# Attention rounds with one value quarter and one relative quarter each, single maxima, and fewer relative columns in the second group of steps

## The chip, the cores and the metric

One Trainium2 chip, one core of it. The metric is the device time of one execution in microseconds. A change of less than 0.2% can't be told from no change by the runs shown here.

## The reference, cut to what matters

Input x is 16 sequences of 512 rows with 128 features. The layer is pre-norm attention with 16 heads of width 8, and after it a shared and expert feed-forward part. All in float32.

```python
rel_pos = arange(L)[None, :] - arange(L)[:, None] + (MAX_LEN - 1)      # L = 512, MAX_LEN = 128
rel_k, rel_v = relative_k[rel_pos], relative_v[rel_pos]                # table of 255 rows; an index is clipped
scores = einsum('bhld,bhrd->bhlr', Q, K) * scale + einsum('bhld,lrd->bhlr', Q, rel_k)
attn = softmax(scores)
out = einsum('bhlr,bhrd->bhld', attn, V) + einsum('bhlr,lrd->bhld', attn, rel_v)
x = x + out @ Wo.T + bo
x = x + ffn(layernorm(x))      # 2 shared and 8 experts, top 2
```

The table has 255 rows, and an index beyond its end takes the last row. So every key that lies 127 or more ahead of a query's row takes the table's last row: such a key is called far, all others near. For a query in rows 0 to 127 all keys from 256 on are far, for rows 128 to 255 all keys from 384 on; for later queries no block of 128 keys is far as a whole.

## The kernel before, in words

Attention works on a pair of sequences at a time (8 pairs), and within a pair in 16 steps of 32 query rows. A step is 8 quads: a quad is 4 query rows of both sequences and all 16 heads, which is 128 partitions by 512 keys of scores in one PSUM bank. A step has two rounds (j = 0 and 1) of 4 quads in banks 0 to 3. Four steps share a group (`s // GROUP_STEPS`), since they share which key blocks are far: steps 0 to 3 are group 0, 4 to 7 group 1, and so on (the change's title counts from one, so its "group two" is group 1 here). A round is written (s, j) below.

In a round TensorE does in this order (`score_round`, L1287):

1. the scores of four quads: `low_terms` (L1198, two quads at a time on halves of the rows), then per two quads `first_terms` (L1182) for both and `relative_terms` (L1190) for both. Each is four matmuls on the four column quarters of the array, and the last of `relative_terms` counts up `score_done`;
2. products of an earlier step into bank 7 (`AV_BANK`): in j = 0 `relative_products` of step s - 2 (both halves), in j = 1 `value_products` of step s - 1 (both sequences). Columns 0 to 255 of the bank hold the value products, 256 to 511 the relative ones. `relative_products` has as many key blocks as are near: 2 in group 0, 3 in group 1, else 4;
3. in some rounds a piece of the work for the next pair (`AHEAD`: transposed rows in (8, 0) and (8, 1), keys in step 9, queries in 11, natural queries in 12, relative queries in (14, 1) and (15, 0)) or of this pair (`OWN`: values in (0, 1) and (1, 0)), through bank 1 or banks 0 and 1;
4. in j = 1 the transpose of the reduced relative result of step s - 2, into columns 256 to 383 of bank 7;
5. the transposes of the probabilities of the round before (16 of 128 x 128, L1248). The last of them waits (`next_scores_wait`, L1116) until banks 0 to 3 are free for the next scores: all four exponentials of this round done, a piece read, and the first transposed bank copied out.

VectorE takes the maxima of the round (`maxima`, L785: one quad, one quad, then two quads in one instruction), in j = 0 then a copy of transposed probabilities, the two maskings of bank 7 (`mask_products`, L799), another copy and `reduce_relative`; in j = 1 `reduce_values`, `rel_out` and two copies. It has work for the next pair behind these in some rounds: statistics in (4, 1) and (5, 1), variances in (6, 0), normalising in step 7, key and query parts from (10, 1) to (14, 0). ScalarE does the four exponentials (L579) and two copies (L568). GpSimd spreads the queries into masked stationary operands one step ahead. Each engine runs this order as written out; semaphores are the only link.

SP issues for each step the load of `rv_step` (`value_window`, L302, 512 KB, one buffer, free again once `av_done` of the step before is up), then the stores of `rel_t`; before step 11 it adds the copies of keys, and before step 14 those of queries (`copy_queries`, L316), which wait for GpSimd and for ScalarE's and VectorE's splits.

`k_hi`, `k_lo`, `k_both` and `k_swap` hold per sequence the 512 plain keys in columns 0 to 511 and behind them the 256 far ones (blocks 2 and 3 with the table's last row added). `near_keys` and `columns` (L1176, L1179) read in group 0 the plain blocks 0 and 1 and then the far ones, as two stretches; all other groups read the 512 plain ones. `relative_terms` streams 256 columns in group 0 and 512 in all others. `value_products` reads `v_far` (values with the table's last row added) for far blocks, in group 1 too.

After the last pair comes `last_step` (L1332) and then the feed-forward part of all 16 sequences.

Of the kernel before, what the change touches and what calls it, by code (L numbers as in the profile page):

```python
# [45 lines left out]
MAXIMA = 3  # L46
# [13 lines left out]
NEAR_GROUP = RT - FAR  # L60
# [27 lines left out]
def attention_ffn(nc, x, w_qkv, cols, rows, wo_t, bo, rk_win, rv_win, rw, rb, w1, w2, b2,  # L88
                  sw1, sw2, sb2, b1_cols, consts, rel_scratch, out):
    with ExitStack() as ctx:  # L90
# [173 lines left out]
        def _(sp):  # L264
# [74 lines left out]
            def pair_windows(pair, parity, first, ahead):  # L339
# [181 lines left out]
        def _(act):  # L521
# [11 lines left out]
            def high_keys(pair, parity, b):  # L533

                act.wait_ge(k_ready, START + pair * 2 + b + 1)
                plain = q_f[:, b * L:(b + 1) * L]
                nc.scalar.activation(k_hi[parity][:, b, 0:L], plain, ACT.Identity, bias=bks_col[:, 0:1])
                nc.scalar.activation(k_hi[parity][:, b, L:KEYS], plain[:, FAR * P:L], ACT.Identity, bias=bk_far_col[:, 0:1]).then_inc(hi_ready, 1)
# [31 lines left out]
            def exponentials(pair, parity, s, j, first):  # L570
# [131 lines left out]
        def _(dve):  # L702
# [42 lines left out]
            def low_keys(pair, parity, b):  # L745
# [3 lines left out]
                nc.vector.scalar_tensor_tensor(k_lo[:, b, 0:L], plain, bks_col[:, 0:1], k_hi[parity][:, b, 0:L], ALU.add, ALU.subtract)  # L749
                nc.vector.scalar_tensor_tensor(k_lo[:, b, L:KEYS], plain[:, FAR * P:L], bk_far_col[:, 0:1], k_hi[parity][:, b, L:KEYS],  # L750
# [71 lines left out]
            def rel_out(pair, s):  # L822
# [4 lines left out]
                nc.vector.tensor_copy(rel_t[:, s % 2, :], ps[0:64, AV_BANK, 2 * P:3 * P]).then_inc(rel_t_ready, 1)  # L827
# [254 lines left out]
        def _(pe):  # L1082
# [93 lines left out]
            def near_keys(rows, group):  # L1176
                return rows.rearrange("k (a c) -> k a c", c=FAR * P)[:, 0::2, :] if group == 0 else rows[:, 0:L]

            def columns(rows, group):  # L1179
                return rows.rearrange("p (a c) -> p a c", c=FAR * P) if group == 0 else rows  # L1180

            def first_terms(parity, s, q):  # L1182
                group = s // GROUP_STEPS
                for b in range(2):
                    for half in range(2):
                        at = b * 64 + half * 32
                        nc.tensor.matmul(columns(ps[at:at + 32, q % IN_ROUND, :], group), stat_hi[s % 2][:, half, b, q, :],  # L1187
                                         near_keys(k_both[parity][:, half, b, :], group), start=False, stop=False, skip_group_check=True)

            def relative_terms(s, q):  # L1190
                near = FAR * P if s // GROUP_STEPS == 0 else L
                window = L - QT - ROWS * s - QT * q
                for g in range(4):
                    last = nc.tensor.matmul(ps[32 * g:32 * g + 32, q % IN_ROUND, 0:near], stat_rel[s % 2][:, q, g, :, :].rearrange("k l h -> k (l h)"),  # L1194
# [3 lines left out]
            def low_terms(parity, s, p):  # L1198

                group = s // GROUP_STEPS  # L1200
                for q, source in ((2 * p, k_hi[parity]), (2 * p + 1, k_swap[parity])):
                    for b in range(2):
                        for half in range(2):
                            at, row = b * 64 + half * 32, 64 * (half ^ (q % 2))
                            nc.tensor.matmul(columns(ps[at:at + 32, q % IN_ROUND, :], group), stat_lo[s % 2][row:row + 64, b, q, :],  # L1205
                                             near_keys(source[row:row + 64, b, :], group), start=True, stop=False, skip_group_check=True)

            def scores(parity, s, j):
# [3 lines left out]
                for p in duos:  # L1212
                    for q in (2 * p, 2 * p + 1):
# [341 lines left out]
```

## Time and profile before

| what | value |
|---|---|
| median of 3 runs | 2220.38 us (2219.79 to 2220.86) |
| the profiled execution: its time | 2220.67 us |
| its span, first to last instruction | 2218.6 us |
| mean granted TensorE clock | 0.990 |
| TensorE busy | 2116.2 us (95%) |
| VectorE busy | 1700.0 us (77%) |
| ScalarE busy | 1522.2 us (69%) |
| GpSimd busy | 1059.8 us (48%) |
| attention rounds | about 44 us to 1676 us of the span |

The span and the time differ by 2.1 us, so what is saved within the span is saved in the time. A TensorE matmul row counts to its modelled end, so "busy" says little; the weight loads (PEld) have real starts, and the start of a round is the start of its first load of `low_terms` (L1205). Times in rows of a timeline are from the start of the span.

### The profile page before, as it was taken

The page shows a single profiled execution, that of the slowest core. Times are in us where ns is not written, and L with a number is a line of the kernel's source. Part 1 is how long each engine was busy: PE and PEld are TensorE (multiplying, and loading weights), DVE is VectorE, ACT ScalarE, POOL GpSimd, SP SyncE. Part 2 cuts the span into 40 slices and gives each one's busy share as a digit, 9 for nine tenths or more (in the row PEclk, how much of TensorE's full clock was granted, in tenths as well). Part 3 has the DMA queues.
Part 4 walks back from the last instruction along what each step waited for, and adds up shares of the span by engine and source line. Part 5 has one row for each costly group of instructions (what it writes and reads, how often), then busy time and mean ns, then how long its engine had stood idle before and what let it go on. Part 6 is the DMA issues. An engine that isn't in the chain of part 4 may idle for free.

```text
span 2218.6 us, 87983 instructions
## 1 busy us (share of the span) xinstructions
PE 2116.2 (95%) x37442; PEld 1547.3 (70%) x37442; DVE 1700.0 (77%) x3703; ACT 1522.2 (69%) x3290; POOL 1059.8 (48%) x992
## 2 busy tenths in 40 slices
PE   3999999999999999999999999999998999999998
PEld 1667767676677667767776777777776777777776
DVE  4787887888788888888787888788875676766665
ACT  3666666666666666666666666666665888888887
POOL 2444344345334433443444335334332777776776
PEclk7999999999999999999999999999999999999999
DMA  5112211321221122112212211222112122122110
GB/s 135 32 53 65 71 53 43 83 58 47 65 71 53 46 70 73 43 53 73 62 53 59 76 53 43 64 62 62 53 43 40 22 24 28 19 28 24 27 21 11
DMA packets 255678, 114.46 MB, mean 52 GB/s; under 512 B 142218, under 2 KB 251156, under 8 KB 255348
## 3 DMA queue, kind: packets, MB, share of 16 engines
q1 hardware_dynamic: 255348, 109.60, 20.5%
q8 instruction: 264, 4.33, 0.8%
q14 instruction: 66, 0.54, 0.1%
HBM read 83.34 MB, written 8.39 MB: 41 GB/s over the span
## 4 chain that ended last, share of the span: by engine, by line
PE 67%; DVE 15%; ACT 9%; issue 4%; POOL 3%; SPq 1%; DMA 0%; ACTq 0%; POOLq 0%; DVEq 0%
PE ps L1248 14%; PE ps L1187 9%; PE ps L1265 9%; PE ps L1194 7%; DVE neg_max L789 6%; PE ps L1205 6%; PE ps L1277 5%; ACT probs L579 4%; POOL probs_t L500 3%; DVE probs_t L795 3%; ACT probs L646 2%; PE ps L1431 2%; PE ps L1414 2%; PE ps L1416 2%; PE ps L1415 2%
## 5 line engine op out<-in xcount | busy, mean ns | idle before, releaser
L579 ACT ACTIVATE probs<-ps,neg_max 128x512 f32<-128x512 f32 x1024 | 694.3, 683 | 467.2 <-DVE neg_max L789 467.2
L789 DVE TENSOR_REDUCE neg_max<-ps 128x1 f32<-128x512 f32 (+1 forms) x768 | 619.1, 861 | 157.8 <-PE ps L1194 157.4
L439 POOL TENSOR_TENSOR stat_hi<-q_twice,mask8h 128x1024 f16<-128x1024 f16 x128 | 243.6, 1903 | 879.2 <-PE ps L1194 773.2
L1248 PE MATMUL ps<-const,probs 128*128 128x128 f32 x4096 | 513.7, 275 | 33.8 <-DVE probs_t L795 18.4
L1248 PEld LDWEIGHTS ps<-const,probs 128*128 128x128 f32 x4096 | 455.8, 142 | 84.0 <-ACT probs L579 36.5
L795 DVE COPY probs_t<-ps 128x512 f32<-128x512 f32 x512 | 339.9, 684 | 89.2 <-PE ps L1248 86.5
L500 POOL TENSOR_TENSOR probs_t<-probs,probs_t 128x1024 f16<-128x1024 f32 x160 | 340.1, 2134 | 109.0 <-ACT probs_t L652 109.0
L568 ACT ACTIVATE probs_t<-ps 128x512 f32<-128x512 f32 x512 | 283.9, 595 | 96.4 <-PE ps L1248 95.4
L1187 PE MATMUL ps<-keys,stat_hi 128*32 128x512 f16 x4096 | 314.4, 383 | 0.0
L1194 PE MATMUL ps<-rk_split,stat_rel 96*32 96x512 f16 (+1 forms) x4096 | 284.3, 353 | 0.0
L999 DVE SCALAR_TENSOR_TENSOR keys<-ps,comb,keys 128x128 f32<-128x128 f32 x640 | 179.8, 344 | 129.3 <-PE ps L1433 129.3
L455 POOL TENSOR_TENSOR stat_rel<-q_rel,mask4h 96x1024 f16<-96x1024 f16 x128 | 250.6, 1958 | 34.1 <-DVE q_rel L774 34.1
L646 ACT ACTIVATE probs<-ps,b_s 128x512 f32<-128x512 f32 x320 | 205.2, 683 | 54.0 <-PE ps L1416 50.7
L1431 PE MATMUL ps<-w_h,probs_t 128*128 128x128 f16 x1280 | 222.8, 219 | 5.2 <-DVE keys L999 1.8
L1433 PE MATMUL ps<-w_h,probs_t 128*128 128x128 f16 x1280 | 222.6, 219 | 0.0
L1432 PE MATMUL ps<-w_l,probs_t 128*128 128x128 f16 x1280 | 222.6, 219 | 0.0
L1265 PE MATMUL ps<-probs_t,v_s 128*32 128x128 f32 x6656 | 215.5, 272 | 0.0
L1277 PE MATMUL ps<-probs_t,rv_step 128*32 128x128 f32 x6656 | 204.1, 272 | 0.0
L579 ACT ACTIVATION_READ_ACCUMULATOR probs<-ps,neg_max 128x1 f32 x1024 | 200.7, 196 | 0.0
L1265 PEld LDWEIGHTS ps<-probs_t,v_s 128*32 128x32 f32 x6656 | 184.9, 110 | 20.3 <-issue 0.2
L1277 PEld LDWEIGHTS ps<-probs_t,rv_step 128*32 128x32 f32 x6656 | 183.9, 110 | 20.2 <-issue 0.2
L1187 PEld LDWEIGHTS ps<-keys,stat_hi 128*32 128x32 f16 x4096 | 85.4, 95 | 151.0 <-issue 107.6
(136 smaller groups left out, 2867.4 us busy)
## 6 DMA issues: line engine op xcount, KB each, us to landing
rv_step<-in_rv_win SPq DMA_DIRECT2D x128, 512.0 KB, 3.8
keys<-keys SPq DMA_DIRECT2D x64, 96.0 KB, 2.3
x_pair<-in_x SPq DMA_DIRECT2D x8, 512.0 KB, 4.3
q_twice<-q_hi SPq DMA_DIRECT2D x32, 128.0 KB, 2.4
q_lo_pair<-q_lo SPq DMA_DIRECT2D x32, 128.0 KB, 2.4
rel_scratch<-rel_t SPq DMA_DIRECT2D x256, 16.0 KB, 3.2
x_pair<-in_x SPq DMA_DIRECT2D x16, 256.0 KB, 3.0
x_pair<-rel_scratch SPq DMA_DIRECT2D x64, 64.0 KB, 3.9
```

The source lines that it names most:

```text
L455: nc.gpsimd.tensor_tensor(stat_rel[s % 2][:].rearrange("k q g l h -> k (q g) l h"), quads.unsqueeze(2).broadcast_to([REL_K, QUADS * 4, QT, ...
L500: nc.gpsimd.tensor_tensor(hid_l[:, n % SLOTS, :, :], hid[:, n % 2, :, :], hid_h[:, n % SLOTS, :, :], ALU.subtract).then_inc(hid_low, 1)
L568: nc.scalar.activation(probs_t[s % 2][:, q, :, :].rearrange("p r c -> p (r c)"), ps[:, tr_bank(q, piece), :], ACT.Copy).then_inc(evac_act, 1)
L579: nc.scalar.activation(probs[:, q, :], ps[:, i, :], ACT.Exp, bias=neg_max[:, q:q + 1], accum_out=row_sum[parity][:, s * QUADS + q:s * QUAD ...
L789: nc.vector.tensor_reduce(neg_max[:, IN_ROUND * j + at:IN_ROUND * j + at + n], ps[:, at:at + n, :], op=ALU.max, axis=AX_X, negate=True).th ...
L795: nc.vector.tensor_copy(probs_t[s % 2][:, q, :, :].rearrange("p r c -> p (r c)"), ps[:, tr_bank(q, piece), :]).then_inc(evac_dve, 1)
L1187: nc.tensor.matmul(columns(ps[at:at + 32, q % IN_ROUND, :], group), stat_hi[s % 2][:, half, b, q, :], near_keys(k_both[parity][:, half, b, ...
L1194: last = nc.tensor.matmul(ps[32 * g:32 * g + 32, q % IN_ROUND, 0:near], stat_rel[s % 2][:, q, g, :, :].rearrange("k l h -> k (l h)"), rk_s ...
L1248: last = nc.tensor.transpose(ps[:, bank, rt * P:(rt + 1) * P], probs[:, q, rt * P:(rt + 1) * P], ident)
L1265: nc.tensor.matmul(ps[32 * g:32 * g + 32, AV_BANK, b * P:(b + 1) * P], values[:, 32 * g:32 * g + 32], cols, start=rt == 0, stop=rt == RT - ...
L1277: last = nc.tensor.matmul(ps[32 * g:32 * g + 32, AV_BANK, (2 + half) * P:(3 + half) * P], rv_step[:, RT - 1 - rt, q * 32:q * 32 + 32], pro ...
L1431: nc.tensor.matmul(y, hid_h[:, place, k, rows], w2_h[:, e, k, :], start=k == 0, stop=False)
```

## The change: what it does, and the diff

- `maxima` takes the four quads of a round one by one, four instructions instead of three, and each exponential waits for its own.
- Keys are laid with the far ones first: far 2, far 3, plain 0 to 3. Group 0 reads the columns from 0, group 1 those from 128 (far 3, plain 0 to 2), later groups those from 256, always 512 in one stretch. So the quads of groups 0 and 1 have the far keys first in the bank, and `relative_terms` writes the last columns: 256 in group 0, 384 in group 1 (before 512), 512 later. The key blocks in `value_products` and `relative_products` are counted accordingly; their number is as before.
- In group 0 the first two quads of a round go first, relative, first, relative.
- The products: round (s, 0) does the value products of sequence 1 and the relative half 1 of step s - 2, round (s, 1) the value products of sequence 0 and the relative half 0 of step s - 1. `av_done` comes in (s, 0) as before. The wait for the landed window is now in (s, 1). `last_step` is rearranged in the same way.
- The transpose of the reduced relative result goes to columns 384 to 511 of bank 7.
- SP issues `copy_queries` in step 14 behind the window and the stores.

```diff
-                    if ahead and s == STEPS - 2:
-                        copy_queries(pair + 1, False)
                     if s:
                         value_window(pair, s - 1)
...
                             copy_keys(pair + 1, 1 - parity, b)
+                    if ahead and s == STEPS - 2:
+                        copy_queries(pair + 1, False)
...
-                    if i < MAXIMA:
-                        act.wait_ge(max_done, START + ((pair * STEPS + s) * ROUNDS + j) * MAXIMA + i + 1)
+                    act.wait_ge(max_done, START + pair * TILES + s * QUADS + q + 1)
...
-                for at, n in ((0, 1), (1, 1), (2, 2)):
-                    dve.wait_ge(score_done, START + pair * TILES + s * QUADS + IN_ROUND * j + at + n)
-                    nc.vector.tensor_reduce(neg_max[:, IN_ROUND * j + at:IN_ROUND * j + at + n], ps[:, at:at + n, :], op=ALU.max, axis=AX_X,
-                                            negate=True).then_inc(max_done, 1)
+                for i in range(IN_ROUND):
+                    q = IN_ROUND * j + i
+                    dve.wait_ge(score_done, START + pair * TILES + s * QUADS + q + 1)
+                    nc.vector.tensor_reduce(neg_max[:, q:q + 1], ps[:, i, :], op=ALU.max, axis=AX_X, negate=True).then_inc(max_done, 1)
...
+            def group_keys(rows, group):
+                start = min(group, RT - FAR) * P
+                return rows[:, start:start + L]
+
+            def group_blocks(group):
+                far = [(block, True) for block in range(min(RT, group + FAR), RT)]
+                return far + [(block, False) for block in range(RT - len(far))]
...
             def relative_terms(s, q):
-                near = FAR * P if s // GROUP_STEPS == 0 else L
+                near = min(RT, s // GROUP_STEPS + FAR) * P
...
                 for p in duos:
-                    for q in (2 * p, 2 * p + 1):
-                        first_terms(parity, s, q)
-                    for q in (2 * p, 2 * p + 1):
-                        relative_terms(s, q)
+                    if s < GROUP_STEPS and p % 2 == 0:
+                        for q in (2 * p, 2 * p + 1):
+                            first_terms(parity, s, q)
+                            relative_terms(s, q)
+                    else:
+                        for q in (2 * p, 2 * p + 1):
+                            first_terms(parity, s, q)
+                        for q in (2 * p, 2 * p + 1):
+                            relative_terms(s, q)
...
                     pe.wait_ge(rel_reduced, START + pair * STEPS + s)
+                else:
+                    pe.wait_ge(rel_t_ready, START + pair * STEPS + s)
...
                 scores(parity, s, j)
-                if j == 0:
-                    before, step = (pair, s - 2) if s >= 2 else (pair - 1, STEPS + s - 2)
-                    if s >= 2 or not first:
-                        for half in range(2):
-                            relative_products(before, step, half)
-                else:
-                    for b in range(2):
-                        if s:
-                            value_products(pair, s - 1, b)
-                        elif not first:
-                            value_products(pair - 1, STEPS - 1, b)
+                trailing = s - 2 + j
+                if trailing >= 0:
+                    value_products(pair, trailing, 1 - j)
+                    relative_products(pair, trailing, 1 - j)
+                elif not first:
+                    value_products(pair - 1, STEPS + trailing, 1 - j)
+                    relative_products(pair - 1, STEPS + trailing, 1 - j)
```

## Rows read from the trace of the kernel before

**Rows 1.** The page's busy time, share of the span and instructions of each engine.
```profile
PE 2116.2 (95%) x37442; PEld 1547.3 (70%) x37442; DVE 1700.0 (77%) x3703; ACT 1522.2 (69%) x3290; POOL 1059.8 (48%) x992
```

**Rows 2.** Windows: steps 6, 7, 8 of pair 3; stretch, length, busy time per engine.
```profile
733.11:744.94 11.83, 11.83 (x242) 8.51 (x242) 10.56 (x31) 7.88 (x21) 5.76 (x5) 1.00 0.17 48
744.94:756.98 12.04, 12.01 (x242) 8.54 (x241) 10.14 (x22) 7.90 (x21) 6.53 (x10) 1.00 0.17 50
756.98:770.46 13.48, 12.79 (x250) 9.38 (x249) 11.35 (x20) 8.81 (x23) 5.44 (x7) 1.00 0.16 44
```

**Rows 3.** Timeline of step 2 (group 0), pair 3: start, duration, engine, line, [idle before].
```profile
686.91 0.14 PEld L1205 LDWEIGHTS ps<-keys,stat_lo 64*32 64x32 f16 x16 [0.17 <-issue]
...
688.24 2.42 DVE L789 TENSOR_REDUCE neg_max<-ps 128x1 f32<-128x512 f32 x3 [1.25 <-PE ps L1194]
...
688.67 0.89 PEld L1277 LDWEIGHTS ps<-probs_t,rv_step 128*32 128x32 f32 x32
...
689.71 0.68 ACT L579 ACTIVATE probs<-ps,neg_max 128x512 f32<-128x512 f32 x1
689.90 0.40 SPq L307 DMA_DIRECT2D rv_step<-in_rv_win  x1
...
690.62 0.69 DVE L795 COPY probs_t<-ps 128x512 f32<-128x512 f32 x1
690.70 0.69 ACT L579 ACTIVATE probs<-ps,neg_max 128x512 f32<-128x512 f32 x1 [0.22 <-DVE neg_max L789]
...
692.20 0.14 PEld L1248 LDWEIGHTS ps<-const,probs 128*128 128x128 f32 x1 [0.65 <-ACT probs L579]
...
692.45 0.14 PEld L1205 LDWEIGHTS ps<-keys,stat_lo 64*32 64x32 f16 x16
...
696.24 1.78 PEld L1248 LDWEIGHTS ps<-const,probs 128*128 128x128 f32 x16
...
698.18 0.10 PEld L1205 LDWEIGHTS ps<-keys,stat_lo 64*32 64x32 f16 x5 [0.17 <-issue]
```

**Rows 4.** Timeline of step 4 (group 1), pair 3.
```profile
709.47 0.14 PEld L1205 LDWEIGHTS ps<-keys,stat_lo 64*32 64x32 f16 x16 [0.17 <-issue]
...
711.55 0.99 PEld L1277 LDWEIGHTS ps<-probs_t,rv_step 128*32 128x32 f32 x32
...
715.12 0.14 PEld L1205 LDWEIGHTS ps<-keys,stat_lo 64*32 64x32 f16 x16
715.68 0.12 PEld L1187 LDWEIGHTS ps<-keys,stat_hi 128*32 128x32 f16 x8 [0.42 <-issue]
...
721.28 0.14 PEld L1205 LDWEIGHTS ps<-keys,stat_lo 64*32 64x32 f16 x16 [0.17 <-issue]
```

**Rows 5.** VectorE's instructions in rows by form, 300 to 1800 us: busy, mean ns.
```profile
L789 DVE TENSOR_REDUCE neg_max<-ps 128x1 f32<-128x512 f32 x432 | 277.8, 684 | 121.5 <-PE ps L1194 121.1
L789 DVE TENSOR_REDUCE neg_max<-ps 128x2 f32<-128x1024 f32 x216 | 262.2, 1214 | 0.0
```

**Rows 6.** Timeline: rounds of pair 3 where VectorE is late or holds the bank.
```profile
673.21 1.27 DVE L795 COPY probs_t<-ps 128x512 f32<-128x512 f32 x2
...
674.26 0.14 PEld L1205 LDWEIGHTS ps<-keys,stat_lo 64*32 64x32 f16 x16
...
740.64 2.41 DVE L789 TENSOR_REDUCE neg_max<-ps 128x1 f32<-128x512 f32 x3
...
752.75 2.41 DVE L789 TENSOR_REDUCE neg_max<-ps 128x1 f32<-128x512 f32 x3
...
759.18 2.41 DVE L789 TENSOR_REDUCE neg_max<-ps 128x1 f32<-128x512 f32 x3
```

**Rows 7.** Landing of `rv_step` loads: of 26 (500 to 840 us), and of the one at 847.63.
```profile
DMA to landing us min/median/max: 3.7/3.8/4.2
DMA to landing us min/median/max: 5.1/5.1/5.1
```

**Rows 8.** Timeline of GpSimd at the change of pair.
```profile
858.52 1.96 POOL L455 TENSOR_TENSOR stat_rel<-q_rel,mask4h 96x1024 f16<-96x1024 f16 x1 [4.50 <-DVE q_rel L774]
```

More of the change, by code:

```diff
@@ L59 @@
 KEYS = L + FAR_COLS
-NEAR_GROUP = RT - FAR
 START = 1
@@ L1173, in project_values @@
                 last.then_inc(proj_done, 1)
[L1176 to L1180, printed above, removed]
+            def group_keys(rows, group):
[4 more added lines that the diff above has]
+                return far + [(block, False) for block in range(RT - len(far))]
             def first_terms(parity, s, q):
@@ L1186, in first_terms @@
                         at = b * 64 + half * 32
-                        nc.tensor.matmul(columns(ps[at:at + 32, q % IN_ROUND, :], group), stat_hi[s % 2][:, half, b, q, :],
-                                         near_keys(k_both[parity][:, half, b, :], group), start=False, stop=False, skip_group_check=True)
+                        nc.tensor.matmul(ps[at:at + 32, q % IN_ROUND, :], stat_hi[s % 2][:, half, b, q, :],
+                                         group_keys(k_both[parity][:, half, b, :], group), start=False, stop=False, skip_group_check=True)
             def relative_terms(s, q):
-                near = FAR * P if s // GROUP_STEPS == 0 else L
+                near = min(RT, s // GROUP_STEPS + FAR) * P
                 window = L - QT - ROWS * s - QT * q
                 for g in range(4):
-                    last = nc.tensor.matmul(ps[32 * g:32 * g + 32, q % IN_ROUND, 0:near], stat_rel[s % 2][:, q, g, :, :].rearrange("k l h -> k (l h)"),
+                    last = nc.tensor.matmul(ps[32 * g:32 * g + 32, q % IN_ROUND, L - near:L], stat_rel[s % 2][:, q, g, :, :].rearrange("k l h -> k (l h)"),
                                             rk_split[:, window:window + near], start=False, stop=True, skip_group_check=True)
@@ L1204, in low_terms @@
                             at, row = b * 64 + half * 32, 64 * (half ^ (q % 2))
-                            nc.tensor.matmul(columns(ps[at:at + 32, q % IN_ROUND, :], group), stat_lo[s % 2][row:row + 64, b, q, :],
-                                             near_keys(source[row:row + 64, b, :], group), start=True, stop=False, skip_group_check=True)
+                            nc.tensor.matmul(ps[at:at + 32, q % IN_ROUND, :], stat_lo[s % 2][row:row + 64, b, q, :],
+                                             group_keys(source[row:row + 64, b, :], group), start=True, stop=False, skip_group_check=True)
             def scores(parity, s, j):
@@ L1257, in value_products @@
                     pe.wait_ge(rel_reduced, START + pair * STEPS + s)
+                else:
+                    pe.wait_ge(rel_t_ready, START + pair * STEPS + s)
                 if s == 0:
                     pe.wait_ge(operands_ready, START + pair * 6 + 5 + b)
-                for rt in range(RT):
+                for rt, (block, far) in enumerate(group_blocks(group)):
                     for g in range(4):
@@ L1263, in value_products @@
                         cols = probs_t[s % 2][:, :, rt, at:at + 32].rearrange("p q (l h) -> p q l h", l=QT)[:, :, :, (g % 2) * 4:(g % 2) * 4 + 4]
-                        values = v_s[:, b * 4 + rt, :] if rt < group + FAR else v_far[:, b, rt - FAR, :]
+                        values = v_far[:, b, block - FAR, :] if far else v_s[:, b * 4 + block, :]
                         nc.tensor.matmul(ps[32 * g:32 * g + 32, AV_BANK, b * P:(b + 1) * P], values[:, 32 * g:32 * g + 32], cols,
@@ L1270, in relative_products @@
                 if half == 0:
-                    pe.wait_ge(rel_t_ready, START + pair * STEPS + s)
                     pe.wait_ge(rv_landed, START + (pair * STEPS + s + 1) * 16)
-                for rt in range(near):
+                for block in range(near):
                     for g in range(4):
                         q = half * 4 + g
-                        last = nc.tensor.matmul(ps[32 * g:32 * g + 32, AV_BANK, (2 + half) * P:(3 + half) * P], rv_step[:, RT - 1 - rt, q * 32:q * 32 + 32],
-                                                probs_t[s % 2][:, q, rt, :], start=rt == 0, stop=rt == near - 1, skip_group_check=True)
+                        last = nc.tensor.matmul(ps[32 * g:32 * g + 32, AV_BANK, (2 + half) * P:(3 + half) * P], rv_step[:, RT - 1 - block, q * 32:q * 32 + 32],
+                                                probs_t[s % 2][:, q, RT - near + block, :], start=block == 0, stop=block == near - 1, skip_group_check=True)
                 if half == 1:
@@ L1333, in last_step @@
                 s = STEPS - 1
-                for half in range(2):
-                    relative_products(pair, s - 1, half)
+                value_products(pair, s - 1, 1)
+                relative_products(pair, s - 1, 1)
                 transposes(pair, s, 1, False, None)
@@ L1339, in last_step @@
                 prepare_attention(0, 0, 0)
-                for b in range(2):
-                    value_products(pair, s, b)
+                value_products(pair, s, 0)
+                relative_products(pair, s, 0)
                 rel_transposes(pair, s - 1)
@@ L1344, in last_step @@
                 prepare_output(0)
-                for half in range(2):
-                    relative_products(pair, s, half)
+                value_products(pair, s, 1)
+                relative_products(pair, s, 1)
                 prepare_h(0)
```

13 lines of the change are left out of this document (6 added, 7 removed).

## The prediction

> **What bounds the kernel now.** First the busy line: TensorE is called 95% busy [rows 1], but its ends are modelled, so I went to the starts of rounds instead. The seven pairs after the first keep one rhythm, so pair 3 stands for all. The windows give step lengths [rows 2], and in the timeline of a step the reader should look at what stands just ahead of the next round's first load. In round (2, 0) it is ScalarE: the last transpose stood 0.65 us for the last exponential [rows 3]. In (2, 1) nothing is waited for but 0.17 us of issue: TensorE's own stream sets the round. So the two rounds of a step are unequal: one short of TensorE work and set by maxima and exponentials, the other set by TensorE.
>
> TensorE's stream, from loads [rows 3, 4]. Scores take 688.67 - 686.91 = 1.76 us in group 0 (256 relative columns) and 711.55 - 709.47 = 2.08 with 512. Value and relative loads take 0.89 us per 32, thus 0.028 each; right after 512-column scores 32 take 0.99. A value quarter is 32 loads, a relative half 8 per near block. Then 0.20 of issue, and from the first transpose to the next round 698.18 - 696.24 = 1.94; j = 1 has 0.06 more for the small transpose. Check: (2, 1) = 1.76 + 64 x 0.0277 + 0.20 + 0.06 + 1.94 = 5.73, and the rows say 698.18 - 692.45 = 5.73. (4, 1): 2.08 + 1.87 + 0.26 + 1.94 = 6.15; the rows say 6.16.
>
> The other chain: let T be the first maximum's start after the round's. (2, 0) has T = 1.33 and length 5.54, so T + 4.21. Inside it exponential 1 starts at T + 1.47, but exponential 2 at T + 2.46, for it waits 0.22 us for the double maximum [rows 3].
>
> **The change, part by part.**
>
> *Single maxima.* Two single ones take 0.60 to the next start and 0.68 to the end, 1.28 against 1.21 for the double one [rows 3, 5]: VectorE pays 0.07 a round, 256 x 0.07 = 18 us if it were always on the path. The exponentials gain: number 2 follows number 1 at T + 1.47 + 0.67 = T + 2.14 instead of T + 2.46. So this chain becomes T + 3.9.
>
> *384 columns.* 32 quads of group 1 per pair lose 128 columns on four matmuls side by side. Group 0 gives the price of 256 columns: scores and the first 32 loads behind them take 1.76 + 0.89 = 2.65 there and 2.08 + 0.99 = 3.07 with 512 [rows 3, 4]. Half of the 0.42 is 0.21 a round; 64 rounds, 13 us as far as TensorE sets the round, nothing where it doesn't. Scores and 32 loads of group 1 then take 2.86, scores alone about 1.9.
>
> *Products.* Each round now has 32 value loads and 16, 24 or 32 relative ones. TensorE's floor in group 0 is 1.76 + 48 x 0.028 + 0.20 + 1.94 = 5.23 (j = 0) and 5.29 (j = 1); in group 1 with two near blocks 2.86 + 16 x 0.028 + 0.20 + 1.94 = 5.45 and 5.51, with three (24 loads more instead of 16) 5.67 and 5.73. Groups 2 and 3 keep 64 loads in each round: nothing.
>
> Next, whether VectorE lets these floors stand. In j = 0 it copies when the first transposes are in: 690.62 - 689.56 = 1.06 after the last product load [rows 3], about 0.9 where TensorE goes on after 0.2, and it is free for the next maxima 2.4 us later. New (2, 0): product loads end at 3.09, so copy at 3.99, free at 6.4, which is T = 1.17 in (2, 1): chain T + 3.9 = 5.1, below 5.29. In j = 1 the first copy starts at T + 3.0 (four maxima 2.41, `reduce_values` 0.38, `rel_out` 0.20), and from that copy to the next round it is 674.26 - 673.21 = 1.05 where it holds the bank [rows 6]: T + 4.05 = 5.2 in (2, 1) and 5.4 in (4, 1). Both just hold.
>
> Per pair, lengths before to after:
> - (1, 1) 5.73 to 5.36 (T is about 1.3 there, after the value pieces, an estimate); (2, 0) and (3, 0) 5.54 to 5.23; (2, 1) and (3, 1) 5.73 to 5.29: -0.37 - 0.62 - 0.88 = -1.87. (0, 0) to (1, 0) still carry products of the pair before with four near blocks, 64 loads: nothing.
> - (4, 0), (5, 0) 5.66 to 5.45; (4, 1) 6.16 to 5.51; (5, 1) 6.16 to 5.73: -1.50. (6, 0), (7, 0): 5.66 to 5.67, since they get 56 loads for 48. (6, 1): VectorE comes late from the variances, at a place that TensorE's transposes in (6, 0) fix and that stays; from the maxima to the end of the round it is 744.94 - 740.64 = 4.30 [rows 2, 6], now 4.05. (7, 1), behind normalising, likewise 756.98 - 752.75 = 4.23 to 4.05. Together -1.91.
> - (8, 0): VectorE's own work from the maxima of (7, 1) to these is 759.18 - 752.75 = 6.43 [rows 6], now 6.50 because of the fourth maximum. So (8, 0) pays back what (7, 1) gave and 0.07: +0.25. (8, 1) 56 loads for 64, -0.21; (9, 0) 56 for 48, +0.22. In (13, 0) and (13, 1) the exponentials end the round behind late maxima: -0.3. Together -0.04; pieces in 11, 12, 14 and 15 wait for VectorE at an unchanged place.
>
> Sum -3.82 for seven pairs, -26.7. The last pair has no work for a next one: (6, 1) and (7, 1) reach 5.73 (from 6.17), group 1 gives -2.4, total about -4.25. In all -31. Of this TensorE's removed columns are at most 13; the rest is levelling. The feed-forward part is untouched. 2220.7 - 31 = 2190, and as the profiled execution lies 0.3 above the median, 2190 also against that.
>
> *The transpose's new place and SP's order.* `rel_out` of step s - 2 is done in (s, 1) at about T + 2.8, the new wait in (s + 1, 0) comes 2 us into the next round: nothing. `copy_queries` behind the window starts at about 843 instead of 838.6; its low half waits for VectorE until 845 anyway. GpSimd's spread then ends some 0.3 later, and behind it stands an idle of 4.50 us for `q_rel` [rows 8], which covers it; without the cover it would be 7 x 0.3 = 2 us. Were the order left, the window would be asked for at 847.6 and needed at 846: the move is needed by the new place of `relative_products`.
>
> *The window itself.* SP issues it 0.34 after the last load of the relative products (688.67 + 0.89 to 689.90 [rows 3]). Before, it had a whole step. Now in group 0: last load at 3.09, issue 3.43, landing 3.8 later [rows 7], 7.23; wanted at 5.23 + 1.76 + 0.89 = 7.88. Spare 0.64 us in group 0, likewise 0.78 in group 1 and 0.98 in the rest. The bounds: 3.7 to 4.2 among 26, so nothing; 5.1 behind other traffic, and all at that, 32 x 0.66 + 32 x 0.52 + 64 x 0.32 = 58 us. I take 0, since 4.2 still fits and nothing is queued ahead of it at its new time.
>
> *First, relative, first, relative* in group 0 brings two more changes between 128-row and 96-row matmuls per round. The first maximum can start 0.2 sooner; the chain isn't the limit then, so 0. Where a change of shape costs, the rows show 0.17 to 0.20, and 0.42 from 64-row to 128-row loads [rows 4]; between L1187 and L1194 they show no idle. Bounds 0 and 64 x 2 x 0.42 = 54 us; I take 0.
>
> The Trainium skill, "TensorEngine Tiling (Array Packing)", section Key Properties, says that changing the tiling mode drains TensorE. The trace agrees for 64 to 128 rows (0.42); it doesn't say whether 96 rows are a mode of their own. If they are, 54 us come on top by it and the sum is 2244, else 2190; it is rival C that prices this from rows.
>
> **Rivals.**
> A. *The window decides* (the other side). Place: the first relative product of every (s, 1). It costs from a landing of 4.4 us on and outweighs the gain from about 4.9 (128 x 1.085 - 108 = 31 us). With 5.1 everywhere: 2190 + 58 = 2248. For: one buffer, and one row of 5.1. Against: 26 others of at most 4.2.
> B. *VectorE decides in more rounds.* Step 2 has it at 9.2 us of what will be 10.5, step 6 at 10.6 of 11.6 [rows 2]; maxima that start 0.25 late in the eight rounds j = 1 of groups 0 and 1 cost 8 x 8 x 0.25 = 16: 2206.
> C. *Drains* in group 0: 2 x 0.2 a round, 64 rounds, 26 us: 2216; by 0.42, 2244.
> D. *More gain.* (6, 1), (7, 1) reach TensorE's floor of 5.73 and (8, 0) doesn't pay back: 0.2 + 0.5 + 0.25, times 7: 2183.
>
> **How the numbers follow.** Chances: forecast 0.56 (2186 to 2196), D 0.14, B 0.18, C 0.05 (half of it slower), A 0.07. Predicted 2190. The range goes from D's end to past B, 2181 to 2210; outside lie A, C and a little more. Under 0.2% (4.4 us) the runs can't tell a change. Faster 0.89; same 0.03, from A or C partly true; slower 0.08.
>
> **What would show it.** Right: (2, 0) at 5.2 and (2, 1) at 5.3 in starts of L1205, exponentials without the 0.22 gap, (4, 1) at 5.5, (8, 0) at 7.1, group 3 as before, feed-forward the same. A shows as idle of the relative matmuls with a DMA as releaser; B as transposes waiting for VectorE's copy in j = 1; C as issue idle between first and relative loads in steps 0 to 3. Wrong altogether if a release that I have off the path (stat_ready, `rel_t_ready`) stands in front of many rounds.

## The result, and the profile after

The changed kernel takes 2184.41 us (median of 4 runs, 2182.88 to 2186.30), the one before beside it 2220.09 (2218.94 to 2220.86). The ratio is 0.984, 95% interval 0.9823 to 0.9857: faster by 36 us. Forecast were 2190 and 31 us: the time lies inside the stated range of 2181 to 2210, and 1.6 us below the narrower band of 2186 to 2196 that had the chance of 0.56.

First the page of the kernel after: the busy line, which answers to [rows 1], and the shares of the chain that ended last, after and then before.

```profile
PE 2092.8 (96%) x37442; PEld 1546.1 (71%) x37442; DVE 1704.3 (78%) x3959; ACT 1502.6 (69%) x3290; POOL 1059.9 (49%) x992
...
PE 74%; DVE 9%; ACT 7%; issue 4%; POOL 3%; SPq 1%; DMA 1%; ACTq 0%; POOLq 0%; DVEq 0%
```

```profile
PE 67%; DVE 15%; ACT 9%; issue 4%; POOL 3%; SPq 1%; DMA 0%; ACTq 0%; POOLq 0%; DVEq 0%
```

The busy line hardly moves, with 256 VectorE instructions more and no matmul fewer. The chain says what happened: TensorE's share is up by 7 points, VectorE's is down by 6 and ScalarE's by 2. The span fell from 2218.6 to 2183.6 us.

The same step 2 of pair 3 as in [rows 3], in the timeline of the kernel after, first the weight loads, then VectorE:

```profile
671.13 0.14 PEld L1204 LDWEIGHTS ps<-keys,stat_lo 64*32 64x32 f16 x16
...
672.90 0.45 PEld L1273 LDWEIGHTS ps<-probs_t,v_far 128*32 128x32 f32 x16
673.34 0.45 PEld L1273 LDWEIGHTS ps<-probs_t,v_s 128*32 128x32 f32 x16
673.77 0.45 PEld L1283 LDWEIGHTS ps<-probs_t,rv_step 128*32 128x32 f32 x16
674.42 1.73 PEld L1253 LDWEIGHTS ps<-const,probs 128*128 128x128 f32 x16 [0.20 <-issue]
676.32 0.14 PEld L1204 LDWEIGHTS ps<-keys,stat_lo 64*32 64x32 f16 x16 [0.16 <-issue]
...
681.61 0.14 PEld L1204 LDWEIGHTS ps<-keys,stat_lo 64*32 64x32 f16 x16 [0.17 <-issue]
```

```profile
672.25 2.48 DVE L786 TENSOR_REDUCE neg_max<-ps 128x1 f32<-128x512 f32 x4 [0.90 <-PE ps L1193]
675.12 0.69 DVE L791 COPY probs_t<-ps 128x512 f32<-128x512 f32 x1 [0.38 <-PE ps L1253]
...
677.50 2.48 DVE L786 TENSOR_REDUCE neg_max<-ps 128x1 f32<-128x512 f32 x4
679.89 0.47 DVE L807 TENSOR_REDUCE attn_t<-v_masked 128x32 f32<-128x128 f32 x2
```

(2, 0) is 676.32 - 671.13 = 5.19 us, before 5.54; the 0.65 us ahead of its last transpose is gone, and 16 transposes run in one go to the 0.16 of issue. (2, 1) is 5.29, before 5.73. The first maximum starts at T = 1.12 and 1.18 (T as in the prediction: from the start of the round to its first maximum). The scores take 672.90 - 671.13 = 1.77 us with the new order of first and relative terms, 1.76 before.

From the starts of `low_terms` the length of every round can be listed. Medians over pairs 1 to 6, us; rounds not shown differ by 0.01 or less:

| round | before | forecast | after |
|---|---|---|---|
| (1, 1) | 5.73 | 5.36 | 5.33 |
| (2, 0), (3, 0) | 5.54 | 5.23 | 5.19 |
| (2, 1), (3, 1) | 5.73 | 5.29 | 5.30 |
| (4, 0), (5, 0) | 5.66 | 5.45 | 5.40 |
| (4, 1) | 6.16 | 5.51 | 5.51 |
| (5, 1) | 6.16 | 5.73 | 5.72 |
| (6, 0), (7, 0) | 5.66 | 5.67 | 5.62 |
| (6, 1) | 6.16 | 5.91 | 5.96 |
| (7, 1) | 6.39 | 6.2 | 6.22 |
| (8, 0) | 6.89 | 7.14 | 6.75 |
| (8, 1) | 6.60 | 6.39 | 6.37 |
| (9, 0) | 6.53 | 6.75 | 6.74 |
| (13, 0), (13, 1), (14, 0) | 18.93 | 18.6 | 18.57 |
| a pair | 204.67 | 200.85 | 200.14 |

And there is one wait that was not there before. The waits of the kernel after, and SP's issues around it, in the last pair:

```profile
PEld ps L1283 <- DMA rv_step<-in_rv_win: 2.8, 1, 2.8
```

```profile
1475.55 0.40 SPq L305 DMA_DIRECT2D rv_step<-in_rv_win  x1
1476.45 0.84 SPq L312 DMA_DIRECT2D rel_scratch<-rel_t  x2
1481.24 0.41 SPq L380 DMA_DIRECT2D x_pair<-in_x  x1
1481.69 5.70 SPq L382 DMA_DIRECT2D x_pair<-rel_scratch  x4
1487.44 1.28 SPq L305 DMA_DIRECT2D rv_step<-in_rv_win  x1
```

`first_rel` waits until 1481.24 for the last store of the pair before and then holds SP for 6.2 us. The window comes only at 1487.44, it lands 5.7 us later, and the relative products of (3, 1) stand 2.8 us for it: that round takes 8.00 us in the last pair, for 5.30 in the others.

### The profile page after: what moved, and what is told of

The parts are those of the page before. It is cut to its first block, busy times and chain, and to the rows that moved or that the text cites. A ratio compares the mean times of both kernels' runs of the same rounds, so it can differ in the third digit from the quotient of the medians.

```text
span 2183.6 us, 88119 instructions
## 1 busy us (share of the span) xinstructions
PE 2092.8 (96%) x37442; PEld 1546.1 (71%) x37442; DVE 1704.3 (78%) x3959; ACT 1502.6 (69%) x3290; POOL 1059.9 (49%) x992
## 3 DMA queue, kind: packets, MB, share of 16 engines
HBM read 83.34 MB, written 8.39 MB: 42 GB/s over the span
## 4 chain that ended last, share of the span: by engine, by line
PE 74%; DVE 9%; ACT 7%; issue 4%; POOL 3%; SPq 1%; DMA 1%; ACTq 0%; POOLq 0%; DVEq 0%
PE ps L1253 17%; PE ps L1186 10%; PE ps L1273 9%; PE ps L1283 7%; PE ps L1193 7%; PE ps L1204 6%; POOL probs_t L498 3%; DVE probs_t L791 2%; ACT probs L643 2%; ACT probs L576 2%; PE ps L1434 2%; PE ps L1417 2%; PE ps L1419 2%; PE ps L1418 2%; PE ps L1435 2%
## 5 line engine op out<-in xcount | busy, mean ns | idle before, releaser
L786 DVE TENSOR_REDUCE neg_max<-ps 128x1 f32<-128x512 f32 x1024 | 635.5, 683 | 123.6 <-PE ps L1193 120.9
L1253 PE MATMUL ps<-const,probs 128*128 128x128 f32 x4096 | 506.1, 275 | 21.5 <-DVE probs_t L791 20.2
L1253 PEld LDWEIGHTS ps<-const,probs 128*128 128x128 f32 x4096 | 454.0, 142 | 62.4 <-issue 26.8
L1193 PE MATMUL ps<-rk_split,stat_rel 96*32 96x512 f16 (+2 forms) x4096 | 281.5, 340 | 0.0
L1283 PE MATMUL ps<-probs_t,rv_step 128*32 128x128 f32 x6656 | 226.5, 273 | 2.5 <-DMA rv_step<-in_rv_win 2.5
L1273 PE MATMUL ps<-probs_t,v_s 128*32 128x128 f32 x6656 | 226.3, 272 | 0.0
L576 ACT ACTIVATION_READ_ACCUMULATOR probs<-ps,neg_max 128x1 f32 x1024 | 207.3, 202 | 0.0
L1186 PEld LDWEIGHTS ps<-keys,stat_hi 128*32 128x32 f16 x4096 | 91.3, 96 | 158.1 <-issue 108.2
L447 POOL TENSOR_TENSOR stat_lo<-q_lo_pair,mask8h 128x128 f16<-128x128 f16 x512 | 188.2, 399 | 0.0
```

Source lines behind the costliest of these rows:

```text
L576: nc.scalar.activation(probs[:, q, :], ps[:, i, :], ACT.Exp, bias=neg_max[:, q:q + 1], accum_out=row_sum[parity][:, s * QUADS + q:s * QUAD ...
L786: nc.vector.tensor_reduce(neg_max[:, q:q + 1], ps[:, i, :], op=ALU.max, axis=AX_X, negate=True).then_inc(max_done, 1)
L1186: nc.tensor.matmul(ps[at:at + 32, q % IN_ROUND, :], stat_hi[s % 2][:, half, b, q, :], group_keys(k_both[parity][:, half, b, :], group), st ...
L1253: last = nc.tensor.transpose(ps[:, bank, rt * P:(rt + 1) * P], probs[:, q, rt * P:(rt + 1) * P], ident)
L1273: nc.tensor.matmul(ps[32 * g:32 * g + 32, AV_BANK, b * P:(b + 1) * P], values[:, 32 * g:32 * g + 32], cols, start=rt == 0, stop=rt == RT - ...
L1283: last = nc.tensor.matmul(ps[32 * g:32 * g + 32, AV_BANK, (2 + half) * P:(3 + half) * P], rv_step[:, RT - 1 - block, q * 32:q * 32 + 32], ...
```

## The experiments

All but the last two start from the changed kernel. "A pair" is the difference of the median pair to its 200.14 us. Times are medians, and "+12" is the distance to the 2184.41 us of the changed kernel; the kernel before ran beside each, and in brackets stands the ratio to it with its 95% interval. Where two of these intervals overlap, the rows decide and not the time.

### Three maxima again

```diff
-                for i in range(IN_ROUND):
-                    q = IN_ROUND * j + i
-                    dve.wait_ge(score_done, START + pair * TILES + s * QUADS + q + 1)
-                    nc.vector.tensor_reduce(neg_max[:, q:q + 1], ps[:, i, :], op=ALU.max, axis=AX_X, negate=True).then_inc(max_done, 1)
+                for at, n in ((0, 1), (1, 1), (2, 2)):
+                    dve.wait_ge(score_done, START + pair * TILES + s * QUADS + IN_ROUND * j + at + n)
...
```

> The changed kernel with the maxima of a round in three instructions again (one, one, two quads). Theory (rounds of groups 0 and 1 are levelled so that TensorE's stream and the chain maxima - exponentials end almost together): the chain is 4.2 us from the first maximum to the next round instead of 3.9, so rounds whose chain then outlasts TensorE get longer: (2, 0) 5.19 to 5.33, (4, 0) 5.40 to 5.60, (4, 1) and (6, 1) by 0.1, (13, 0) by 0.3; together about 1.3 us a pair, +10 us (2194). Groups 2 and 3 otherwise as they are. Rival (single maxima only cost VectorE 0.07 a round and TensorE decides everywhere): no change or 2 to 5 us faster.

2196.67 us (ratio to before 0.9894, 0.9878 to 0.9911): +12. A pair +1.77. (2, 0) 5.33, (4, 0) 5.60, (4, 1) 5.62, (13, 0) 6.45, as expected; (6, 1) +0.20 where 0.1 stood, (7, 1) and (1, 1) +0.20 where nothing stood, (8, 0) -0.11. In its trace the double maximum's gap is back, and behind it the last transpose waits for an exponential:

```profile
677.39 2.42 DVE L786 TENSOR_REDUCE neg_max<-ps 128x1 f32<-128x512 f32 x3 [1.16 <-PE ps L1194]
...
679.85 0.69 ACT L577 ACTIVATE probs<-ps,neg_max 128x512 f32<-128x512 f32 x1 [0.22 <-DVE neg_max L786]
...
681.35 0.14 PEld L1254 LDWEIGHTS ps<-const,probs 128*128 128x128 f32 x1 [0.16 <-ACT probs L577]
```

One more instruction on an engine that is 78% busy is worth 12 us: the rival, by which single maxima only cost, is refuted.

### 512 relative columns in group 1 again

```diff
-                start = min(group, RT - FAR) * P
+                start = 0 if group == 0 else FAR_COLS
...
-                near = min(RT, s // GROUP_STEPS + FAR) * P
+                near = FAR * P if s // GROUP_STEPS == 0 else L
```

> The changed kernel, but group 1 reads the 512 plain keys and streams 512 relative columns again (order of its key blocks as before). Theory: 0.21 us a round in the six rounds of group 1 that TensorE sets, less in (6, 1) and (7, 1): 1.3 us a pair, +10 us (2194); group 0 unchanged. Rival (VectorE and ScalarE decide in group 1): under 4 us. Rival (four column quarters do not run side by side): 1024 matmuls by 53 ns, up to +54 us.

2194.15 us (0.9884, 0.9867 to 0.99): +10. A pair +1.52: exactly +0.21 in (4, 0), (4, 1), (5, 0), (5, 1), (6, 0) and (7, 0), nothing in (6, 1) and (7, 1), and +0.22 in (8, 0), which had not been expected: the four normalising instructions ahead of it took 2.30 us here for 2.08 in the changed kernel, which is what the last experiment is about. So the price of columns holds, and VectorE decides where it was said to. Were the four column quarters not streamed side by side, up to +54 us had been expected: refuted.

### The products apart again

```diff
-                trailing = s - 2 + j
...
+                if j == 0:
+                    before, step = (pair, s - 2) if s >= 2 else (pair - 1, STEPS + s - 2)
+                    if s >= 2 or not first:
+                        for half in range(2):
+                            relative_products(before, step, half)
+                else:
...
```

> The changed kernel with the products as before: both relative halves in j = 0, both value quarters in j = 1, and last_step accordingly. Theory: (2, 0) is then set by the chain at 5.0 to 5.1, (2, 1) by TensorE at 5.73: +0.3 a step in group 0; (4, 0) 5.3, (4, 1) 5.95: +0.3; steps 6 and 7 a little shorter (48 loads in j = 0, VectorE decides j = 1): together +1.3 us a pair, +10 us (2194). Rival (levelling gives most of the 36 us): +20 us or more. Rival (only the removed columns and single maxima matter): within 3 us.

2190.27 us (0.9866, 0.9849 to 0.9882): +6. A pair +0.88, and the wait in (3, 1) of the last pair is gone, -2.7 once. (2, 0) 5.00 and (2, 1) 5.74, (4, 0) 5.27 and (4, 1) 5.94. Levelling gives 0.25 us in steps 2 and 3, 0.41 in step 1, 0.30 in step 4 and 0.09 in step 5, and takes back 0.21 in each of steps 6 and 7: (6, 0) is 5.40 apart and 5.62 levelled, as (6, 1) stays at 5.96 either way. Levelling is the smallest of the three gains, not the largest, as the forecast had it ("the rest is levelling"). This is its worth beside the other two parts; what it would give alone on the kernel before was not run.

### No alternation in group 0

```diff
-                    if s < GROUP_STEPS and p % 2 == 0:
+                    if False:
```

> The changed kernel with first, first, relative, relative in group 0 too. Theory: TensorE's stream is the same length; the first maximum starts 0.2 us later, and the chain then passes TensorE's 5.2 to 5.3 by at most 0.1: +0.3 us a pair, +2 us at most (2185 to 2187). Rival (each change between 128-row and 96-row matmuls drains TensorE): 2 x 0.2 us a round less, 26 us faster (2158).

2189.54 us (2185.07 to 2190.60; 0.9857, 0.9841 to 0.9874). The median is 5 us above the changed kernel's, where 2 at most was forecast, but the two intervals overlap. The trace is clearer: a pair +0.25, (2, 0) 5.22 and (2, 1) 5.37 for 5.19 and 5.30, (1, 1) 5.37 for 5.33, nothing outside group 0. All attention rounds together are 2.3 us longer; the rest of the span's 4.1 us lies mostly behind them, in the feed-forward part, which has no part in the edit. So the alternation gives 2 us in the rounds. It costs nothing that shows: the scores take 1.77 us with it and 1.76 without, and taking it out made nothing faster, so rival C is refuted. The four undone parts add to 1.77 + 1.52 + 0.88 + 0.25 = 4.42 of the 4.53 us that a pair gained.

### The window later

```diff
                 sp.wait_ge(av_done, START + pair * STEPS + s)
+                sp.wait_ge(tr_done, START + pair * TILES + s * QUADS + IN_ROUND + 1)
```

> The changed kernel with one more wait of SP ahead of each load of rv_step: until the first quad of the transposes in (s, 0) is done, about 0.65 us later than now. Theory: the load then lands where it is wanted in group 0 (spare 0.64) and 0.1 to 0.3 ahead of it elsewhere: 0 to +3 us (2184 to 2187). Rival (the load is already late or nearly so in most steps): 128 x 0.65 = +80 us or a good part of it.

2190.83 us (2190.53 to 2196.44; 0.9875, 0.9858 to 0.9891): +6. Rounds as they were, save (3, 1) +0.09; single loads landed late (13 waits, 7.1 us in all, 2.7 of them in (3, 1) of the last pair, as before), so for the median landing there was room, for the slow ones not. The load was issued 0.60 us later in most steps, but 1.1 to 2.1 later in steps 1, 8, 9, 11, 12 and 15, where a piece of other work stands ahead of the transposes.

> The same with the wait for the second quad, about 1.1 us later than now. Theory: the relative matmuls of (s, 1) wait 0.46 us in group 0, 0.32 in group 1, 0.12 in the rest: 32 x 0.46 + 32 x 0.32 + 64 x 0.12 = +33 us (2217), less where the round is set by another chain anyway. Rival (a whole us or more of spare, as landings of 3.8 are fast): under +5 us.

2233.66 us (2228.39 to 2243.82; 1.0062, 1.004 to 1.0084): +49, slower than the kernel before. The waits and landings of this kernel, in an execution of 2243.82 us:

```profile
PEld ps L1284 <- DMA rv_step<-in_rv_win: 75.7, 103, 3.8
```

```profile
DMA to landing us min/median/max: 3.6/4.0/6.0
```

By round medians the waits are 0.57 and 0.50 in group 0 (0.46 forecast), 0.40 to 0 in group 1 (0.32), 0 to 0.5 elsewhere (0.12), 3.4 us a pair or 27 in all, near the 33 of the forecast. What is beyond comes from single slow landings, up to 6.0 us, which the forecast had not: two of eight pairs lose over 12 us. A first delay of 0.60 us cost 6 us, the next 0.43 turned the gain into a loss. So the spare time of 0.64 us in group 0, worked out for rival A, was right to about 0.1.

### SP's copies of queries first again

```diff
+                    if ahead and s == STEPS - 2:
+                        copy_queries(pair + 1, False)
                     if s:
                         value_window(pair, s - 1)
```

> The changed kernel with SP's copies of queries ahead of the window load in step 14 again. Theory: the load is asked for only after the low half's copies, about 4 us into (14, 1), lands 5 us later, and (14, 1) waits 6 us for it in each of seven pairs: +42 us (2226), and the rest of the trace as it is. Rival (step 14 has room, the copies cost little): under +10 us.

2235.13 us (1.0074, 1.0057 to 1.009): +51. (14, 1) goes from 8.39 to 15.42, the other rounds of the median pair stay. Waits, SP's issues, and the windows of (14, 0) with what is before it, of (14, 1) and of (15, 0), of this kernel:

```profile
PEld ps L1283 <- DMA rv_step<-in_rv_win: 41.7, 8, 6.6
```

```profile
847.95 2.39 SPq L327 DMA_DIRECT2D q_lo_pair<-q_lo  x4
850.38 0.59 SPq L305 DMA_DIRECT2D rv_step<-in_rv_win  x1
```

```profile
837.50:846.07 8.57, 8.52 (x162) 6.33 (x151) 8.08 (x15) 6.77 (x19) 3.94 (x6) 1.00 0.28 64
846.07:861.37 15.30, 9.51 (x146) 7.07 (x145) 7.24 (x14) 5.15 (x12) 3.32 (x5) 0.78 0.29 73
861.37:869.20 7.83, 7.17 (x149) 5.29 (x149) 4.96 (x9) 4.88 (x11) 1.18 (x1) 1.00 0.26 75
```

The window is asked for 4.3 us into (14, 1), which began at 846.07. In this round of pair 3 TensorE stood 5.27 us for the load, yet the round grew by 6.9. The granted clock tells where the rest is: 0.78 in this round, 1.00 in the rounds on both sides of it, so TensorE worked a part of it, behind its idle time, at the lower level; the 32 relative loads right behind the wait took 1.48 us. All seven pairs that have the wait show it. The forecast of +42 priced the wait and not the clock. The levelled products can't be had without the move in SP's order; the move on the kernel before, by itself, was not run.

### `first_rel` one step later

```diff
-                    if not ahead and s == 2:
+                    if not ahead and s == 3:
                         first_rel()
```

> The changed kernel with first_rel of the last pair (five loads that SP issues for 6.2 us) one step later, behind the window load of step 2. Theory: the one wait of 2.8 us of the relative matmuls for the window in (3, 1) of the last pair goes, since the five loads no longer wait for the last store and are through before the next window: -2.3 us (2182), hardly above noise in the time but plain in the trace. Rival (the loads then hold up the window of the next step instead): the wait moves by a step, no change.

2183.36 us (2181.66 to 2183.47; 0.9831, 0.9815 to 0.9847). Pair 7 falls by 2.88 us, (3, 1) from 8.00 to 5.30, and no wait for the window is left. In the time that is inside the noise.

### VectorE's copies sooner

With the edit before, and:

```diff
+                    copies_first = s in (0, 6, 7, 14)
+                    if copies_first:
+                        evacuate(pair, s, 0, piece)
+                        evacuate(pair, s, 1, piece)
                     if products:
                         reduce_values(*trailing)
                         rel_out(*trailing)
-                    evacuate(pair, s, 0, piece)
-                    evacuate(pair, s, 1, piece)
+                    if not copies_first:
+                        evacuate(pair, s, 0, piece)
+                        evacuate(pair, s, 1, piece)
```

> The changed kernel with first_rel one step later and, in (0, 1), (6, 1), (7, 1) and (14, 1), VectorE's two copies of transposed probabilities ahead of reduce_values and rel_out. Theory (in these rounds the last transpose waits for VectorE's first copy, which stands 0.58 us behind two small operations): (0, 1) 7.50 to 6.92, of which (1, 0) gives a part back since VectorE is late there; (6, 1) 5.96 to TensorE's 5.73; (7, 1) 6.22 to 6.1 (exponentials decide next), which (8, 0) gives back as VectorE's work there is the same; (14, 1) 8.39 to 7.8. About -1.1 us a pair and -2.9 once for first_rel: 2174. Rival (the wait is not for the first copy but for the release of something behind it, or rel_out late holds up the next round): -3 us only, 2182.

2171.86 us (2171.57 to 2174.06; 0.9787, 0.9773 to 0.98). A pair -1.22: (0, 1) 6.92, (14, 1) 7.81, (6, 1) 5.83, (7, 1) 6.10, where 5.73 and 6.1 had been expected for the last two; (8, 0) gives 0.13 back and (1, 0) 0.07.

### GpSimd makes room

With the edits of both before, and:

```diff
+                    if ahead and s == 9:
+                        pool.wait_ge(xn_ready, START + (pair + 1) * 8 + 8)
+                    if ahead and s == 12:
+                        pool.wait_ge(operands_ready, START + (pair + 1) * 6 + 1)
+                    if ahead and s == 14:
+                        pool.wait_ge(q_split_ready, START + (pair + 1) * 4 + 2)
+                    if ahead and s == 15:
+                        pool.wait_ge(operands_ready, START + (pair + 1) * 6 + 3)
                     spread_relative(s)
```

> The kernel of e8, and GpSimd's spread_relative in its steps 9, 12, 14 and 15 waits until VectorE's work for the next pair that it ran beside before (normalising the second half, the first half's k_lo, q_split and q_lo) is done. No instruction is added or taken away. Theory (a VectorE instruction between tiles of SBUF stands still while a GpSimd one runs: over five runs the four normalising instructions took 1.11, 2.08, 2.14, 2.30 and 2.40 us beside 0, 1.22, 1.29, 1.44 and 1.54 us of GpSimd): normalising takes 1.11 and (8, 0) falls from 6.88 to 6.3; k_lo takes 0.75 instead of 2.2 and (11, 0) falls from 7.6 to 6.8; (13, 0) to 6.05; about -1.4 us a pair, 2162. GpSimd's lateness costs nothing, as its result is wanted a round later. Rival (the long durations belong to the instructions and their place, not to GpSimd): durations as they are, no change of time, 2172, or slower by what TensorE then waits for stat_ready.

2166.13 us (2162.95 to 2166.24; 0.9753, 0.974 to 0.9766), the fastest of all. A pair -1.26 against e8: (8, 0) 6.27, (11, 0) 6.95 (6.8 expected), (13, 0) 6.05, (13, 1) +0.06. The time fell by 5.7 us where 10 had been forecast; the attention rounds of this trace are 7.2 shorter than those of the kernel of e8. The rows: VectorE's normalising before, after, and here; k_lo before and here; ahead of each, where it shows, the GpSimd instruction beside it.

Before:

```profile
756.45 1.96 POOL L455 TENSOR_TENSOR stat_rel<-q_rel,mask4h 96x1024 f16<-96x1024 f16 x1
...
756.86 2.40 DVE L742 TENSOR_SCALAR x_pair<-x_pair,mv,rstd 128x128 f32<-128x128 f32 x4
...
795.96 1.96 POOL L455 TENSOR_TENSOR stat_rel<-q_rel,mask4h 96x1024 f16<-96x1024 f16 x1
796.27 2.20 DVE L749 SCALAR_TENSOR_TENSOR k_lo<-q_f,bks_col,keys 128x512 f16<-128x512 f32 x1
```

After:

```profile
733.70 2.48 DVE L786 TENSOR_REDUCE neg_max<-ps 128x1 f32<-128x512 f32 x4
...
735.71 1.47 POOL L447 TENSOR_TENSOR stat_lo<-q_lo_pair,mask8h 128x128 f16<-128x128 f16 x4
736.09 0.47 DVE L807 TENSOR_REDUCE attn_t<-v_masked 128x32 f32<-128x128 f32 x2
...
737.13 1.96 POOL L453 TENSOR_TENSOR stat_rel<-q_rel,mask4h 96x1024 f16<-96x1024 f16 x1
...
737.87 2.08 DVE L739 TENSOR_SCALAR x_pair<-x_pair,mv,rstd 128x128 f32<-128x128 f32 x4
739.88 2.47 DVE L786 TENSOR_REDUCE neg_max<-ps 128x1 f32<-128x512 f32 x4
```

This kernel:

```profile
730.40 1.10 DVE L747 TENSOR_SCALAR x_pair<-x_pair,mv,rstd 128x128 f32<-128x128 f32 x4
...
731.59 1.96 POOL L453 TENSOR_TENSOR stat_rel<-q_rel,mask4h 96x1024 f16<-96x1024 f16 x1 [1.88 <-DVE x_pair L747]
...
768.77 0.74 DVE L754 SCALAR_TENSOR_TENSOR k_lo<-q_f,bks_col,keys 128x512 f16<-128x512 f32 x1
```

GpSimd waits 1.88 us, and nobody waits longer for GpSimd than before (TensorE 4.5 us in all, 4.6 in the kernel of e8); VectorE gets 1.0 us back against the kernel of e8, whose normalising took 2.08 as in the changed kernel (1.3 against the kernel before), and 1.5 for k_lo. One round of the last pair was 0.68 longer in this profile, (4, 1): its relative products waited 0.74 us for the window. `first_rel`, now in step 3, had held SP for 9.4 us, the window was issued right behind it at 1479.66 and landed 5.0 us later. So the rival of the experiment with `first_rel` came true in this execution, at a quarter of the price.

## Why the prediction was right, and where it wasn't

- *Two chains of a round.* Right. TensorE's floors were met to 0.05 us in thirteen rounds; 0.04 of that is the way from the first transpose to the next round in j = 0, 1.90 and not 1.94. T in (2, 1) came out at 1.18 for 1.17.
- *Single maxima.* Right in kind, too small in standing. The forecast never priced the part alone; it is the largest, 12 us, since the double maximum sits on the chain in every round that isn't TensorE's, also where VectorE is late.
- *384 columns.* 10 us for "13 us as far as TensorE sets the round".
- *Levelling.* "The rest is levelling" is the sentence that failed: of the forecast's 31 us it leaves 18 to levelling, and apart again it costs 6 us, or 7 without the wait in (3, 1). With single maxima and fewer columns the short round is already at 5.0, and the other one alone decides.
- *(8, 0).* The term of the sum that failed in size. It was to pay back what (7, 1) gave, +0.25; it fell by 0.14. From maxima to maxima VectorE took 739.88 - 733.70 = 6.18 us, not 6.50. The fourth maximum did cost its 0.07; but normalising went from 2.40 to 2.08, for it ran beside GpSimd's instruction for 1.22 us and not 1.54: GpSimd starts behind the scores of (7, 1), which fewer columns had made shorter, and VectorE came later by the fourth maximum. With 512 columns again the two numbers are 2.30 and 1.44, and the last experiment, with nothing beside it, has 1.10. That is 0.32 of the 0.39 us; the rest lies behind the maxima of (8, 0), 4.60 us to the end of the round for 4.69.
- *The window.* The spare times were right, and "nothing is queued ahead of it at its new time" was true of 127 loads. In (3, 1) of the last pair `first_rel` was queued ahead: rival A in one place, 2.7 us. The prediction went through SP's order in the pairs that prepare a next one, and not in the last.
- *SP's order and the alternation.* Right: needed by 51 us, and worth 2 us.
- *The rivals.* A came true in one round, B nowhere, C not. D (2183) has nearly the measured time, but mostly not its mechanism: (6, 1) and (7, 1) stayed at 5.96 and 6.22 and did not reach 5.73; only (8, 0) did not pay back.
- *The sum.* It came within 5 us partly because errors cancelled. Pairs 1 to 6 gained 26.8 us for 22.9; (8, 0) is 2.3 of the difference, the rest 0.04 here and there. The last pair gained 2.0 for 4.25, as 2.7 went into its wait for the window. Pair 0 gained 6.9 for 3.8, and 2.0 of it lie in its first two rounds, where the windows give the granted clock as 0.50 and 0.56 before and 0.75 and 0.59 after (column before the DMA share):

```profile
44.35:51.30 6.95, 4.13 (x50) 1.42 (x49) 2.51 (x3) 2.89 (x8) 4.67 (x6) 0.50 0.01 2
51.30:60.40 9.10, 8.32 (x81) 5.68 (x82) 4.83 (x7) 3.25 (x9) 5.24 (x6) 0.56 0.00 0
```

```profile
44.74:50.54 5.80, 3.62 (x50) 1.34 (x49) 2.62 (x4) 2.90 (x8) 4.67 (x6) 0.75 0.01 3
50.54:58.80 8.26, 7.91 (x74) 5.66 (x74) 4.93 (x8) 3.23 (x9) 4.83 (x6) 0.59 0.00 0
```

So in these two rounds TensorE, which had been all but idle from 40 to 44 us, goes from the lower of its two levels to the full one, and in the trace after a larger part of them ran at the full one. No part of the change is aimed at this. Whether the change brings it is not shown: the two rounds together take 13.0 to 14.6 us in all eleven traces of changed kernels and 16.0 in the only one of the kernel before. Pair 0 as a whole also varies, 200.6 us in the changed kernel and 201.6 in the one with `first_rel` later, whose pairs 1 to 6 are alike to 0.05.

## What to carry to other kernels

Write a round as the longest of its chains, each in rows of the trace (the engine's own stream; maxima to exponentials to the next use; the copy that frees a bank), and price every edit in each: a reduction split in two was worth a little more here than 1024 shortened matmuls (1.77 us a pair to 1.52), because the consumer of its first half no longer waited for both. When a load's deadline moves nearer, list everything that its queue issues in the step, in each variant of the loop, the last turn too; here the spare was 0.6 us, and issuing the load 0.4 us later than that made the kernel slower than before. When an engine's small operations stand between another engine and the buffer that it wants, put the copy first.

## What the runs showed of the hardware

Some VectorE instructions nearly stand still while a GpSimd instruction runs, and others don't notice it. Four normalising instructions (TENSOR_SCALAR, SBUF to SBUF) took 1.11 us beside none, and 2.08, 2.14, 2.30 and 2.40 beside 1.22, 1.29, 1.44 and 1.54 us of GpSimd, over five kernels and seven pairs each; k_lo (SCALAR_TENSOR_TENSOR, SBUF to SBUF) took 0.74 alone and 2.20 beside 1.65. So they grew by the overlap less 0.2 to 0.3 us. In the same kernels the half of k_lo that no GpSimd instruction runs beside takes 0.74 too, so it isn't the instruction's place alone. But the theory of the last experiment, by which every instruction between tiles of SBUF stands still, is too wide: in the changed kernel the TENSOR_REDUCE of `v_masked` takes 277 ns beside GpSimd and 273 alone, the statistics (BATCH_NORM_STATS2) 274 and 278, and the maxima, which read PSUM, 683 and 682. Which of the two kinds an instruction is has to be read in the trace. Letting GpSimd wait instead brought 5.7 us.

The load of 512 KB landed 3.8 to 4.0 us after its issue in the median of each kernel, the fastest after 3.6, but single ones took up to 6.0, so a spare of under a microsecond is paid for now and then.

A change from 64-row to 128-row matmuls showed 0.42 us of idle weight loads, but changes between 128-row and 96-row ones none: two more of them in a round left the scores at 1.77 us for 1.76.

A wait can cost more than its length: where TensorE stood 5.27 us for a load in (14, 1), its granted clock was 0.78 in that round, against 1.00 in the rounds around it, and the round grew by 6.9 us.
